# A graph layer on one core: the order of loads, transposes and aggregations in its head

## The reference

```python
h = maximum(layernorm(x), 0)                      # per row: (x - mean) / sqrt(var + 1e-5)
type_sum = adj @ h                                # the same matrix for both edge types
attn_a = sigmoid([type_sum, h] @ Wa.T + ba)
attn_b = sigmoid([type_sum, h] @ Wb.T + bb)
g = h @ W_sa
scores = (g @ a_left)[:, None] + (g @ a_right)[None, :]
e = where(adj != 0, exp(-leaky_relu(scores, 0.01)), 0)
x_a = (e / (e.sum(1) + 1e-5)) @ g
x_b = adj @ (h @ W_gcnb) + b_gcnb
out = x + sigmoid(attn_a * x_a + attn_b * x_b)
```

## Time and profile before

| | us |
|---|---|
| median of three runs | 177.93 |
| the profiled execution | 176.94 |
| its span (first to last instruction) | 175.1 |
| PE busy in the span | 170.5 |
| DVE, ACT, POOL busy | 144.5, 113.2, 24.5 |

### The profile page before, as it was taken

How to read it: one execution, slowest core, us unless ns; L and a number is a source line. 1 busy time by engine, 2 the same in 40 slices (tenths; PEclk the granted TensorE clock), 3 DMA queues, 4 the chain that set the end, 5 groups by cost and what they waited for, 6 DMA issues and landing times.

```text
span 175.1 us, 3378 instructions
## 1 busy us (share of the span) xinstructions
PE 170.5 (97%) x1313; PEld 124.6 (71%) x1313; DVE 144.5 (83%) x306; ACT 113.2 (65%) x167; POOL 24.5 (14%) x43
## 2 busy tenths in 40 slices
PE   7999999999999999999999999999999999999992
PEld 2556764455554478888744488888888888888892
DVE  3799995589999995999999703999999999976551
ACT  3769996349868889298658600875875874863310
POOL 4846441002007930000000000000000000000000
PEclk9999999999999999999999999999999999999998
DMA  5999999986999369900010100000010010011101
GB/s 135 296 213 260 226 231 175 207 157 110 215 220 332 146 112 216 247 28 2 0 64 0 60 0 0 4 0 0 4 60 0 6 60 0 4 62 60 64 30 30
DMA packets 9071, 17.66 MB, mean 101 GB/s; under 512 B 3920, under 2 KB 4704, under 8 KB 8288
## 3 DMA queue, kind: packets, MB, share of 16 engines
q0 software_dynamic: 1728, 8.39, 25.0%
q1 hardware_dynamic: 7328, 9.06, 16.3%
HBM read 22.94 MB, written 2.11 MB: 143 GB/s over the span
## 4 chain that ended last, share of the span: by engine, by line
PE 97%; DVE 1%; issue 0%; ACT 0%; DVEq 0%
PE ps L822 32%; PE ps L865 16%; PE ps L863 16%; PE ps L864 16%; PE ps L856 6%; PE ps L797 6%; PE ps L905 3%; PE ps L791 1%; PE ps L926 0%; DVE logit L771 0%; DVE e_lo L557 0%; PE ps L818 0%; ACT logit L434 0%; DVE res L664 0%; DVE e_hi L519 0%
## 5 line engine op out<-in xcount | busy, mean ns | idle before, releaser
L863 PE MATMUL ps<-mv_lo,e_hi 128*128 128x257 f16 (+2 forms) x272 | 71.0, 267 | 0.0
L865 PE MATMUL ps<-mv_hi,e_lo 128*128 128x257 f16 (+2 forms) x272 | 70.9, 266 | 0.0
L864 PE MATMUL ps<-mv_hi,e_hi 128*128 128x257 f16 (+2 forms) x272 | 70.8, 266 | 0.0
L400 ACT ACTIVATE z<-z,log_e 128x1024 f32<-128x1024 f32 x32 | 36.7, 1146 | 31.2 <-DVE z L601 31.2
L601 DVE SCALAR_TENSOR_TENSOR z<-sl_row,exs,far 128x512 f32<-128x512 f32 x64 | 45.1, 746 | 0.6 <-DMA sl_row<-sl_line 0.6
L609 DVE TENSOR_TENSOR e_lo<-z,e_hi 128x1024 f16<-128x1024 f32 x32 | 39.0, 1220 | 1.4 <-ACT e_hi L410 1.4
L822 PE MATMUL ps<-adj,nat_lo 128*128 128x512 f16 x128 | 36.8, 379 | 0.0
L822 PE MATMUL ps<-adj,nat_hi 128*128 128x512 f16 x128 | 36.7, 379 | 0.0
L410 ACT ACTIVATE e_hi<-z 128x1024 f16<-128x1024 f32 x32 | 33.3, 1041 | 0.0
L863 PEld LDWEIGHTS ps<-mv_lo,e_hi 128*128 128x128 f16 x272 | 26.4, 97 | 3.4 <-ACT c_sb L388 0.3
L864 PEld LDWEIGHTS ps<-mv_hi,e_hi 128*128 128x128 f16 x272 | 26.5, 98 | 3.1
(11 more groups left out here) (69 smaller groups left out, 170.0 us busy)
## 6 DMA issues: line engine op xcount, KB each, us to landing
adj<-in_adj_t POOLq DMA_DIRECT2D x6, 1024.0 KB, 9.8
x_sb<-in_x SPq DMA_DIRECT2D x6, 512.0 KB, 8.2
out<-res SPq DMA_DIRECT2D x7, 256.0 KB, 2.0
adj<-in_adj_t POOLq DMA_DIRECT2D x4, 256.0 KB, 6.7
adj<-in_adj_t POOLq DMA_DIRECT2D x2, 512.0 KB, 8.7
x_sb<-in_x SPq DMA_DIRECT2D x3, 256.0 KB, 4.0
sl_row<-sl_line SPq DMA_DIRECT2D x2, 256.0 KB, 5.5
sl_row<-sl_line SPq DMA_DIRECT2D x1, 512.0 KB, 7.0
```

The lines of the kernel that those rows point to most:

```text
L400: act.activation(z[:, n % ZRING, :, :], z[:, n % ZRING, :, :], ACT.Exp, bias=log_e[:, 0:1], scale=SLOPE - 1.0).then_inc(exp_done, 1)
L863: pe.matmul(ps[:, bank, cols], e_hi[:, s, i1], mv_lo[:, j, cols], start=(j == 0), stop=False)
L864: pe.matmul(ps[:, bank, cols], e_hi[:, s, i1], mv_hi[:, j, cols], start=False, stop=False)
L865: return pe.matmul(ps[:, bank, cols], e_lo[:, s, i1], mv_hi[:, j, cols], start=False, stop=(j == NT - 1))
```

## The change

- SP issues x part 0, `consts`, x part 1, `w_wide`, x part 2, x part 3. x part 6 waits for x part 5 and no longer for a piece of the adjacency; `w_post` and `rows` are loaded after the first piece of adjacency chunk 2; `sl_spread(0)` waits for the first piece of chunk 1.
- TensorE runs five fillers, the score product (as soon as `consts` is there), one filler, and then the units 0 and 1. The other six fillers are gone.
- For units 0 and 1 ScalarE no longer scales: it writes relu(x - mean) (`centred`), and 1/deviation comes in by a diagonal matrix that VectorE makes (`diagonal`). `turn_scaled` is a float32 matmul with it in place of the transpose with `ident`. `nat_hi` and `nat_lo` of these tiles take the factor when they are written (`first_nat_highs`, `first_nat_lows`).
- The high half of `wa` is made by ScalarE. The tiles 0 and 1 have two of three parts of their wide product ahead of `b_pair(0)`, the third after it. The two-column products for tile 0 are gone.
- POOL makes the variance and the negated mean from unit 4 on; its loads of the adjacency pieces 3 to 6 come one norm later in its list.
- `nat` halves come ahead of the evictions of the wide product on ScalarE and VectorE; wide(4) and wide(5) are done after `b_pair(6)`; the wide product of tiles 8 and 9 uses the banks 0 and 1; the second row of scores goes to bank 3 and is transposed within `b_products(1, ...)`; `w_post`'s halves are made at n = 8 and 9 of the main loop.

The core of the diff:

```diff
-WARM = 7
+WARM = 5
-SL_BANKS = (6, 6, 0)
+SL_BANKS = (6, 3, 0)
+POOL_FROM = 4
+NCENTRED = 2
-WIDE_BANKS = (6, 2, 6, 2, 6, 2, 0, 2)
+WIDE_BANKS = (6, 2, 6, 2, 0, 2, 0, 2)
+        diag = res[:, 0, :, 0:P]
...
             load_x(0)
+            sp.dma_start(c_sb[:, :], consts).then_inc(c_landed, 16)
             load_x(1)
+            sp.dma_start(wa_sb[:, :, :], w_wide).then_inc(wa_landed, 16)
             load_x(2)
-            sp.dma_start(wa_sb[:, :, :], w_wide).then_inc(wa_landed, 16)
-            sp.dma_start(c_sb[:, :], consts).then_inc(c_landed, 16)
             load_x(3)
...
-            sp.wait_ge(adj_landed[1], 16)
+            sp.wait_ge(x_landed[5], 16)
             load_x(6)
-            sp.wait_ge(x_landed[6], 16)
-            sp.dma_start(wg_sb[:, :, :], w_post).then_inc(wg_landed, 16)
-            sp.dma_start(r_sb[:, :], rows).then_inc(rows_landed, 16)
...
             sl_store(0)
+            sp.wait_ge(adj_landed[piece_of(1, 0)], 16)
             sl_spread(0)
-            sp.wait_ge(adj_landed[piece_of(0, NT - 1)], 16)
...
             sp.wait_ge(adj_landed[piece_of(2, 0)], 16)
+            sp.dma_start(wg_sb[:, :, :], w_post).then_inc(wg_landed, 16)
+            sp.dma_start(r_sb[:, :], rows).then_inc(rows_landed, 16)
...
-                pool.wait_ge(var_ready, u + 1)
+                if u < POOL_FROM:
+                    pool.wait_ge(var_ready, u + 1)
+                else:
+                    pool.wait_ge(moments_done, UNITS[u][1])
+                    pool.tensor_scalar(var_s[:, ts], mean_var[:, ts, 1], LN_EPS, H_SCALE ** -2, ALU.add, ALU.mult).then_inc(var_ready, 1)
+                    pool.tensor_scalar(neg_mean[:, ts], mean_var[:, ts, 0], -1.0, None, ALU.mult).then_inc(neg_ready, 1)
+                    pool.wait_ge(var_ready, u + 1)
                 pool.tensor_tensor(rstd[:, ts], var_s[:, ts], power[:, 0:UNITS[u][1] - UNITS[u][0]], ALU.pow).then_inc(rstd_ready, 1)
+                if u < NCENTRED:
+                    return
...
             norms(2)
             load_adj(2)
+            norms(3)
             load_adj(3)
-            norms(3)
+            norms(4)
             load_adj(4)
-            norms(4)
+            norms(5)
             load_adj(5)
-            norms(5)
+            norms(6)
             load_adj(6)
-            norms(6)
...
+            def centred(u):
+                act.wait_ge(centre_ready, u + 1)
+                act.activation(x_sb[:, u, :], x_sb[:, u, :], ACT.Relu, bias=neg_mean[:, u:u + 1], scale=1.0).then_inc(h0_done, 1)
...
+            def first_nat_highs():
+                act.wait_ge(h0_done, NCENTRED)
+                act.wait_ge(rstd_ready, NCENTRED)
+                for t in range(NCENTRED):
+                    ins = act.activation(nat_hi[:, t, :], x_sb[:, t, :], ACT.Copy, scale=rstd[:, t:t + 1])
+                ins.then_inc(nat_high, 1)
...
-            h0_tiles(0)
-            h0_tiles(1)
+            centred(0)
+            w_wide_high()
+            centred(1)
             h0t_highs(0)
+            first_nat_highs()
             h0t_highs(1)
             h0_tiles(2)
-            nat_highs(0)
             nat_highs(1)
             h0t_highs(2)
             h0_tiles(3)
+            nat_highs(2)
+            h0_tiles(4)
+            h0t_highs(3)
+            nat_highs(3)
             mv_highs(0)
...
+            def diagonal(u):
+                if u == 0:
+                    dve.wait_ge(ident_ready, 3)
+                dve.wait_ge(rstd_ready, u + 1)
+                dve.tensor_scalar(diag[:, u, :], ident[:, :], rstd[:, u:u + 1], None, ALU.mult).then_inc(diag_ready, 1)
...
             moments(0)
-            moments(1)
-            moments(2)
-            w_wide()
+            dve.wait_ge(x_landed[1], 16)
+            stats_of(1)
+            aggregates(1)
+            diagonal(0)
+            last_steps(1)
+            w_scores()
+            dve.wait_ge(x_landed[2], 16)
+            stats_of(2)
+            diagonal(1)
+            stats_of(3)
+            w_wide_low()
+            aggregates(2)
+            last_steps(2)
+            first_nat_lows()
+            moments(3)
             h0t_lows(0)
-            w_scores()
+            moments(4)
+            nat_lows(1)
             h0t_lows(1)
-            moments(3)
-            nat_lows(0)
+            h0t_lows(2)
+            nat_lows(2)
...
+            def turn_scaled(u):
+                pe.wait_ge(diag_ready, u + 1)
+                pe.wait_ge(h0_done, u + 1)
+                for k in range(KT):
+                    ins = pe.matmul(turn_bank(u)[:, 0, k, :], x_sb[:, u, k * P:(k + 1) * P], diag[:, u, :], start=True, stop=True)
+                ins.then_inc(turned, 1)
...
                 if j0 == 0 and c == 1:
-                    pe.wait_ge(mv_ready, 2 * ONTIME)
+                    pe.wait_ge(mv_ready, 6)
+                    pe.wait_ge(sl_moved, 1)
...
             warm(WARM)
-            pe.wait_ge(stats_done, 1)
-            warm(1)
-            pe.wait_ge(var_ready, 1)
-            warm(2)
-            pe.wait_ge(norm_ready, 1)
-            warm(1)
-            pe.wait_ge(ident_ready, 3)
-            turn(0)
-            warm(1)
-            turn(1)
-            pe.wait_ge(wa_high, 1)
-            pe.wait_ge(h0t_high, 1)
-            wide_part(0, slice(0, WG), ((0, 0),))
             pe.wait_ge(c_landed, 16)
...
             ins.then_inc(wl_product, 1)
-            pe.wait_ge(wa_low, 1)
-            wide_part(0, slice(0, WG), ((0, 1),))
+            warm(1)
+            turn_scaled(0)
+            turn_scaled(1)
+            pe.wait_ge(wa_high, 1)
+            pe.wait_ge(wa_ready, 1)
+            for t in range(NCENTRED):
+                pe.wait_ge(h0t_high, t + 1)
+                wide_part(t, slice(0, WA), ((0, 0),))
+                pe.wait_ge(wa_low, 1)
+                wide_part(t, slice(0, WA), ((0, 1),))
+            b_pair(0)
+            turn(2)
             pe.wait_ge(h0t_ready, 1)
-            wide_part(0, slice(0, WG), ((1, 0),))
-            wide(1)
-            wide_part(0, slice(WG, WA)).then_inc(wide_product, 1)
-            turn(2)
-            b_pair(0)
-            for p in range(1, NPAIR):
-                b_pair(p)
-                if p + 2 < NTURN:
-                    turn(p + 2)
-                if p + 1 < NTURN:
-                    wide(p + 1)
-            b_products(1, 0, 8)
+            wide_part(0, slice(0, WA), ((1, 0),)).then_inc(wide_product, 1)
+            b_pair(1)
+            turn(3)
+            wide_part(1, slice(0, WA), ((1, 0),)).then_inc(wide_product, 1)
+            wide(2)
+            b_half_pair(2, 0)
+            turn(4)
+            b_half_pair(2, 1)
+            b_pair(3)
+            turn(5)
+            wide(3)
+            b_pair(4)
+            b_pair(5)
+            b_pair(6)
+            wide(4)
+            wide(5)
+            b_pair(7)
+            b_products(1, 0, 3)
+            pe.wait_ge(mv_ready, 8)
+            sl_lines(1)
+            b_products(1, 3, 8)
+            pe.wait_ge(sl_moved, 2)
             wide(6)
```

More of the change, by code:

```diff
@@ L476, in _ @@
                     sl_lines(2)
+                    act.wait_ge(wg_landed, 16)
+                    act.activation(wg_hi[:, :, :], wg_sb[:, :, :], ACT.Copy, scale=W_SCALE).then_inc(wg_high, 1)
                 if n in (8, 9, 11, 12):
@@ L557, in h0t_lows, with first_nat_lows @@
                 dve.tensor_tensor(h0t_tiles(h0t_lo, u), turn_bank(u), h0t_tiles(h0t_hi, u), ALU.subtract).then_inc(h0t_ready, 1)
+            def first_nat_lows():
+                dve.wait_ge(nat_high, 1)
+                for t in range(NCENTRED):
+                    ins = dve.scalar_tensor_tensor(out=nat_lo[:, t, :], in0=x_sb[:, t, :], scalar=rstd[:, t:t + 1],
+                                                   in1=nat_hi[:, t, :], op0=ALU.mult, op1=ALU.subtract)
+                ins.then_inc(nat_ready, 1)
             def nat_lows(p):
@@ L720, in _ @@
                     agg_lows(1)
+                if n == 9:
+                    w_post_low()
                 if n == 10:
@@ L810, in wide @@
                         pe.wait_ge(mv_ready, t - 3)
-                    if u in SL_UNITS and t == UNITS[u][0]:
-                        sl_lines(SL_UNITS.index(u))
+                    if t == UNITS[SL_UNIT][0]:
+                        sl_lines(0)
                     wide_part(t, slice(0, WA)).then_inc(wide_product, 1)
```

125 lines of the change are left out of this document (73 added, 52 removed).

## The result

| | before | after |
|---|---|---|
| median (lowest to highest) of 6 runs, us | 177.84 (177.00 to 178.66) | 183.56 (180.28 to 185.21) |
| profiled execution, us | 176.94 | 184.50 |
| its span, us | 175.1 | 182.7 |
| PE busy, us | 170.5 | 174.0 |
| instructions | 3378 | 3373 |

The change makes the kernel slower: the ratio is 1.0229, 95% interval 1.0178 to 1.0280. The runs' mean granted clocks are 1.000 and 0.999 in those of 180.28 and 181.27 us, 0.991 in those of 182.83, 184.28 and 184.50 (the profiled one), and 0.980 in that of 185.21.

A forecast was written before the change was run, and what follows sets the result against it. PE, busy 170.5 of 175.1 us, was taken as the bound, so only the head could win. `b_pair(0)` at 9.65 against 9.39 (+0.26) plus 0.1 for piece 5 gave +0.35: 178.3 us on the median 177.93, range 177.0 to 180.1.

The forecast's parts named there:

- The mark and the break-even: Start of chunk 1, 31.01 us before the change; to keep it, `b_pair(0)` must start at 9.39 us.
- Constants at 4.3: In the head, `consts`, now second in the loads, lands at 4.3 us instead of 6.5.
- The score product from there at 0.2 us a step: PE makes the score product from 4.3 us at 1.2 GHz, taking 1.6 to 1.7 us, to 6.0.
- the rival that the constants don't come earlier: Transfers share engines evenly, `consts` stays at up to 6.5 us, all from the score product moves 2 us: 179.9; chance 0.04.
- A float32 matmul of 128 columns at two transposes' time: Each `turn_scaled` matmul costs two transposes: a unit takes 0.45 us at 2.4 GHz, 0.85 at 1.2.
- x part 2 at 6.5: In the head's loads, x part 2, now last, lands at 6.5 us, 1.5 us later than before.
- I take 9.65, since ...: Chosen start of `b_pair(0)`, between 9.4 (early clock rise) and 10.05 (still 1.2 GHz), because PE is less loaded than before.
- the lower clock lasts: Rival: idle holes in the head keep PE at 1.2 GHz until 12.4 or 14.9 us: 179.8 or 181.0; chance 0.20.
- A piece of adjacency is late: Rival: adjacency piece 5 at 25.9 us and piece 1 0.5 us late cost +0.9 to +2.7, middle 179.4; chance 0.10.
- What I cost at nothing: ... the later `sl_spread(0)`: Later score-row spread, and `w_post`'s later load and halves, cost nothing: VectorE idles 2.07 us at 70.23, absorbing two us.
- `turn(2)`, `b_pair(1)`, the steps given to POOL: After `b_pair(0)`, no PE loss: operands at 11.05 for 11.4, adjacency at 11.7 for 12.0; POOL's path 0.3 to 0.4 longer.
- Faster, 0.18: Rival: `b_pair(0)` by 9.3 or a varying head wait removed, up to 1.7 us gained, middle 176.9; chance 0.18.

The follow-up runs named there:

- e3: Changed kernel with two more fillers at the start, two between the first scaled transposes, and the first row's spread not waiting for chunk 1's adjacency; 179.85 us, ratio 1.0126.
- e11: Old kernel with only the change's head (early loads, diagonals, order up to `b_pair(0)`) plus the added fillers of e2; 181.11 us, ratio 1.0212.
- e14: Changed kernel with POOL loading chunk 2's first adjacency piece ahead of its wait for the DMA transposes; 186.18 us, ratio 1.0516.
- e1: Changed kernel without the added wait: the first score row's spread no longer waits for chunk 1's first adjacency piece; 180.10 us, ratio 1.0113.
- e4: Old kernel with five fillers at the start and none of the others, no waits between them; 180.47 us, ratio 1.0167.
- e6: Changed kernel with the added fillers of e2 and two DMA-turned units between the first score row's store and spread; 182.14 us, ratio 1.0283.
- e8: Old kernel with the first score row's store held back until the seventh pair of low halves is ready; 181.22 us, ratio 1.0196.
- e12: Changed kernel with the fillers of e2, the first score row taken out early, and the spread edit of e1; 179.43 us, ratio 1.0118.
- e2: Changed kernel with two more fillers at the start and two between the first two scaled transposes; 180.19 us, ratio 1.0123.
- e9: Changed kernel with the fillers of e2 and the first score row taken out early (`wide(3)` ahead of `b_pair(3)`), SP's list untouched; 180.15 us, ratio 1.0164.

## Why the prediction was wrong

The forecast was 178.3 us, and the range reached to 180.1; the median is 183.56. Point by point:

- **The mark and the break-even** held. With `b_pair(0)` 1.56 late and 1.39 longer, chunk 1 comes within 0.14 of where the arithmetic puts it, and in e3 within 0.02.
- **Constants at 4.3**: measured 4.17 at PE. **The score product from there at 0.2 us a step**: 4.17 to 5.90, 1.73 where 1.6 to 1.7 was said. Right, and with it the rival that the constants don't come earlier falls.
- **A float32 matmul of 128 columns at two transposes' time**: at the lower level, and with no hole ahead of it, `turn_scaled(1)` took 0.86 in e11 (8.04 to 8.90); the estimate was 0.85 (1.02 in the new kernel, 8.19 to 9.21, after a hole). The factor 2 is right, and the four times of the Trainium skill, "TensorE: Matmul & The Clock Gate", section Terms (1.7 us at this level), isn't what this chip did.
- **x part 2 at 6.5**: measured 7.5. Part 0 was 0.5 late in this run too (3.48 where it was 2.96), but in e3 part 0 is on time and x part 2 still comes at 7.0; over the runs with this order of loads it comes between 6.72 (e14) and 7.93 (e1). By itself this puts `turn_scaled(1)` at 8.19, not 7.3, and `b_pair(0)` at 10.95, not 10.05.
- **"I take 9.65, since ..."**: here the choice failed. The rival *the lower clock lasts* is what happened: the level rose at 13.77, between the 12.4 and the 14.9 that I had worked out for it. I gave it 0.20. The row for 1.2 GHz at the score product, the hole of 1.0 us and the lack of any work without a hole before 9.2 all stood in the text, and against them only that "the holes are short, and work at half speed closes them". e4 shows what fewer fillers and a hole do without any other part of the change. The rival's price was +1.85 to +3.1 us; the profile has 1.56 + 1.39 = 2.95 for the head, but 0.9 of it is x part 2 and not the clock. That 180.28 and 181.27 us lie at the rival's 179.8 to 181.0 is partly luck: those runs have no profile, and the rival knew nothing of chunk 2.
- **A piece of adjacency is late**: the rival named pieces 5 and 1. Piece 1 was on time, piece 5, issued at 20.28 where I had 17.3, was late in e1 (0.55, ahead of `b_pair(6)`) and not in the new kernel. The piece that binds is 3, which I had not followed. I had moved `norms(2)` with x part 2 for PE's and VectorE's sake and not asked what stands behind it on POOL's list. It is worth 2.07 us (e3) and 1.55 (e6), in e11 2.03 by way of piece 2, and is hidden in the new kernel by the clock. An estimate for x part 2 at 6.5, as forecast: piece 3 would be issued 1.0 us earlier, at 11.4, and with the 6.6 us of the new kernel or the 8.3 of e3 land at 18.0 or 19.7; a PE at 2.4 GHz with `b_pair(0)` at 9.65 wants it at 18.1 (18.3 in e3). So +0.35 would have needed the quick landing.
- **"What I cost at nothing: ... the later `sl_spread(0)`"**: this is the largest step that failed. The head alone, 2.8 us at chunk 1, would already have made it 180.7, past the range; this adds 4.5 us in the profiled run. I named VectorE's 2.07 us as its cover and looked at the row's reader alone. The queue that the edit passes through has six transposes behind the spread, POOL behind those, and chunk 2 with 0.5 us of margin behind POOL. What sets the spread was wrong as well: not the added wait (0.5 us at the most, e1), but the row itself, which PE makes 5.1 us later and ScalarE copies 7.6 us later, and which the prediction didn't count as a moved step at all. Price: 2.85 us, and 1.64 of the lower clock behind it where that falls; 3.50 by itself on the old kernel (e8).
- **`turn(2)`, `b_pair(1)`, the steps given to POOL**: no wait of PE in the trace, as said. But ScalarE waits 0.81 us for POOL's `shift` on its way to the row's copy, so the steps given to POOL stand in the late chain; their share of it isn't measured.
- **Faster, 0.18**: none of the six runs is under any run of before.

The sum that would have been right: +1.56 for the head, +1.39 for the clock (or +2.07 for piece 3 instead of the clock and most of the head), +2.85 for piece 8 and 1.64 for the clock behind it. The parts do not add: taking away the clock's share brings piece 3's, and what is late at chunk 1 gives piece 8 more time. By the medians no single edit gave back more than 3.5 of the 5.7 us, and three together (e12) 4.1; by the ratios e1 alone, e2 alone, both together (e3) and e12 all stand at 1.1 to 1.3% of loss where the change has 2.3%. So the edits together win no more than one of them.

What stays open: no run has x part 2 early, the row early and the fillers whole at once with the change's other parts kept, so whether the scaled transposes themselves win anything isn't shown. They have not been seen to win.

## What to carry to other kernels

When a transfer is moved later in a queue that is worked through in order, write down everything behind it in that queue, and who waits for each of these, until a consumer with a measured margin is reached; its first reader is not enough. A wait can't be priced at nothing by the slack of one engine if another engine stands in the same chain. Fillers have to last until the first work that has no holes in it (in e3, e6 and e11 they did, in e2, e9 and e12 they didn't and the clock fell again), and work that waits for a late load isn't such work; and a head that is late for one reason may be hiding a second one, so take the first away before you believe that it was the only one.
